# Rows of gathered edges taken from the count tables, jobs spread over three written-out hops, slots unpacked in halves

## What is computed

```python
h = maximum(layernorm(x), 0)
for i in range(10):                       # the hops
    agg = segment_sum(feat[src] * e[:, None], dst)
    feat = (0.9 * agg + 0.1 * h) * r[i] + (1 - r[i]) * feat
x = x + feat
emb = maximum(layernorm(x), 0)
for _ in range(4):                        # the GNN steps
    m = (emb @ W_msg.T + b_msg).reshape(n, 4, 128)
    r = segment_sum(m[src, etype], dst)
    emb = gru_cell(r, emb)
out = x + emb
```

## Time and profile before

| | us |
|---|---|
| median of three runs | 2313.57 (2311.01 to 2314.75) |
| the profiled execution | 2312.61, span 2311.1 |
| PE busy | 2077.3 (90%) |
| DVE busy | 1374.2 (59%) |
| POOL busy | 915.8 (40%) |
| ACT busy | 506.0 (22%) |

### The profile page before, as it was taken

One profiled execution on the slowest core, in us unless ns is written; L12 is line 12 of the kernel. 1 busy time (PEld: TensorE's weight loads), 2 busy tenths in 40 slices (PEclk: granted clock), 3 DMA queues, 4 the chain that ended last, 5 costly groups with the idle time before them and its releaser, 6 DMA issues.

```text
span 2311.1 us, 43556 instructions
## 1 busy us (share of the span) xinstructions
PE 2077.3 (90%) x15432; PEld 1452.2 (63%) x16039; DVE 1374.2 (59%) x2749; ACT 506.0 (22%) x1139; POOL 915.8 (40%) x1021
## 2 busy tenths in 40 slices
PE   3656666799999999999899999999999999999998
PEld 2333333699998989988755566555665556655566
DVE  8989898887776777777752245522455224552233
ACT  3888888300000000000121012210122101220001
POOL 4776775000000000000038870388703887038870
PEclk8665555699999999999999999999999999999999
DMA  2000000100000000001441110411104111043111
GB/s 80 23 24 34 24 34 30 45 1 1 2 2 2 1 2 1 2 2 60 126 125 39 39 44 3 125 40 39 44 3 126 40 39 44 2 127 66 40 44 31
DMA packets 62758, 90.05 MB, mean 39 GB/s; under 512 B 31953, under 2 KB 48927, under 8 KB 59654
## 3 DMA queue, kind: packets, MB, share of 16 engines
q1 hardware_dynamic: 21185, 54.88, 7.3%
q0 software_dynamic: 38400, 31.28, 5.8%
q10 hardware_dynamic: 2944, 0.93, 0.2%
HBM read 47.48 MB, written 39.05 MB: 37 GB/s over the span
## 4 chain that ended last, share of the span: by engine, by line
PE 43%; POOL 26%; DVE 16%; issue 9%; DMA 2%; ACT 2%; DVEq 1%; POOLq 1%; ACTq 0%; SPq 0%
PE ps L1033 26%; POOL big L513 24%; PE ps L938 11%; PE ps L822 2%; DVE m_full L1668 2%; DVE m_parts L1661 2%; PE ps L921 2%; DVE marks L1240 2%; DVE dig L1268 1%; DVE big L1270 1%; DMA messages_by_edge_kind<-m_parts 1%; PE ps L904 1%; POOL win_w L475 1%; DVEq L1227 1%; PE ps L866 1%
## 5 line engine op out<-in xcount | busy, mean ns | idle before, releaser
L513 POOL DMA_INDIRECT big<-messages_by_edge_kind,edge_row x480 | 641.4, 1336 | 1169.9 <-DMA messages_by_edge_kind<-m_parts 1024.8
L938 PE MATMUL ps<-slots,m_parts 125*128 125x436 fp8e4 (+1 forms) x5600 | 962.4, 330 | 4.0 <-DVE m_parts L1661 2.9
L938 PEld LDWEIGHTS ps<-slots,m_parts 125*128 125x128 f16 x5600 | 540.7, 98 | 360.1 <-issue 1.3
L1033 PE MATMUL ps<-parts,big 125*128 125x256 f16 x6125 | 673.2, 273 | 10.8 <-DVE parts L1457 4.4
L1033 PEld LDWEIGHTS ps<-parts,big 125*128 125x128 fp8e4 x6125 | 592.9, 98 | 65.2
L1545 DVE TENSOR_SCALAR slots<-big 128x2800 int32<-128x2800 int32 (+1 forms) x112 | 217.0, 1941 | 259.7 <-PE ps L938 253.3
L822 PE MATMUL ps<-hot_pair,weighed 125*128 125x228 f16 x1000 | 218.4, 369 | 140.8 <-ACT weighed L634 69.6
L822 PEld LDWEIGHTS ps<-hot_pair,weighed 125*128 125x128 f16 x1000 | 117.8, 123 | 241.1 <-ACT weighed L634 202.8
L634 ACT ACTIVATE weighed<-marks,win_w 125x128 f16<-125x128 f16 x625 | 194.7, 391 | 59.4 <-DVE marks L1240 58.9
L565 ACT ACTIVATE rs<-rs 125x25 f32<-125x25 f32 (+3 forms) x5 | 1.1, 216 | 712.0 <-DVE rs L1108 712.0
L1473 DVE SCALAR_TENSOR_TENSOR hop_tmp<-ps,coef,g 125x128 f32<-125x128 f32 x250 | 87.4, 350 | 94.0 <-PE ps L1033 90.2
(11 more groups left out here) (230 smaller groups left out, 1570.3 us busy)
## 6 DMA issues: line engine op xcount, KB each, us to landing
messages_by_edge_kind<-m_parts SPq DMA_DIRECT2D x20, 1120.0 KB
packed_counts<-packed SPq DMA_DIRECT2D x16, 625.0 KB, 2.9
big<-messages_by_edge_kind,edge_row POOLq DMA_INDIRECT x480
big<-packed_counts SPq DMA_DIRECT2D x4, 1400.0 KB, 6.4
big<-packed_counts SPq DMA_DIRECT2D x3, 1050.0 KB, 5.8
messages_by_edge_kind<-m_parts SPq DMA_DIRECT2D x20, 130.0 KB
hd<-in_x SPq DMA_DIRECT2D x1, 1562.5 KB
x_again<-in_x SPq DMA_DIRECT2D x1, 1562.5 KB
```

The source lines that it names most:

```text
L513: pool.indirect_dma_start(out=picked[0:CH, r, w, :, :].rearrange("p h f -> p (h f)"), out_offset=None, in_=m_dram[:, :], in_offset=bass.In ...
L938: last = pe.matmul(ps[:, k % 2, 0:SIZES[k] * QD], m_parts[0:Q, a, t, h, :], slots_f8[0:Q, t % 2, 0:SIZES[k], a, 0:QD], start=a == 0 and t ...
L1033: last = pe.matmul(ps[:, n % RING, 0:2 * F], tot_f8[0:Q, c, a, :], both((parts0, parts1)[par], a), start=a == 0, stop=a == TILES - 1)
```

## The change

The numbers for gathered edges are no longer made over all edges and turned. GpSimd stages key, place and weight of the eight pairs' columns instead (three small instructions a pair, in the room of `hot_to`), and `edge_parts`, 15 small instructions of VectorE, works source row and target out of them. GpSimd waits for the rows once ahead of its gathers (`s_rows`). The three window rows are turned and copied together. VectorE's loop covers hops 0 to 5; hops 6, 7 and 8 are written out and carry, in this order, `update_scales`, `edge_parts` and `mark_targets` (behind every second tile from tile 2). `unpack` issues two instructions, one for half of the block's tiles each; of three tiles the first takes one and the second two. Core of the diff:

```diff
-            hot_to = sb("hot_to", [128, PAIRS, GW, PC], U8, b)
+            hot_room = sb("hot_to", [128, PAIRS * GW * PC], U8, b)
...
+        hot_to = hot_room[:, :].rearrange("p (g w n) -> p g w n", g=PAIRS, w=GW)
+        hot_to_f8 = hot_room[:, :].bitcast(F8).rearrange("p (g w n) -> p g w n", g=PAIRS, w=GW)
+        near = hot_room[:, 0:5 * PAIRS * GW * 4].bitcast(F32).rearrange("p (j m) -> p j m", j=5)
+        near_key, near_place, near_weight, near_pair = (near[:, j, :] for j in range(4))
+        near_lane = near[:, 4, :].bitcast(I32)
...
-            pool.wait_ge(s_edges[1], 16)
-            pool.wait_ge(s_edges[2], 16)
-            pool.tensor_scalar(edge_g[0:ROWS, 0, :], edge_i[0:ROWS, 1, :], float(TYPES), None, ALU.mult).then_inc(s_grow4, 1)
-            pool.tensor_copy(edge_g[0:ROWS, 1, :], edge_i[0:ROWS, 2, :]).then_inc(s_grow4, 1)
-            pool.wait_ge(s_grow4, 2)
-            pool.tensor_tensor(edge_g[0:ROWS, 0, :], edge_g[0:ROWS, 0, :], edge_g[0:ROWS, 1, :], ALU.add).then_inc(s_grow, 1)
-            pool.wait_ge(s_grow, 1)
-            pool.wait_ge(s_edges[0], 16)
-            pool.tensor_copy(edge_g[0:ROWS, 1, :], edge_i[0:ROWS, 0, :]).then_inc(s_grow, 1)
-            pool.memset(edge_kind[:, NCH:PAD], 0)
-            pool.memset(edge_to[:, NCH:PAD], NOWHERE)
             pool.iota(iota_to[:, :], [[1, PC]], base=0, channel_multiplier=0, allow_small_or_imprecise_dtypes=True)
-            pool.iota(pair_off[:, :], [[PC, PAIRS]], base=TILES * QD, channel_multiplier=0, allow_small_or_imprecise_dtypes=True)
...
-            pool.wait_ge(s_gtab, 2)
             pool.wait_ge(s_pair, 1)
             for pair in range(PAIRS):
                 lo = pool.value_load(pair_lo[0:1, pair:pair + 1], min_val=0, max_val=NCH)
-                pool.tensor_copy(edge_row[0:CH, pair * GW:(pair + 1) * GW], edge_kind[0:CH, ds(lo, GW)])
-                pool.tensor_tensor(win_to[0:CH, pair * GW:(pair + 1) * GW], edge_to[0:CH, ds(lo, GW)],
-                                   pair_off[0:CH, pair:pair + 1].broadcast_to([CH, GW]), ALU.subtract).then_inc(s_to, 1)
+                at, q = slice(pair * GW, (pair + 1) * GW), QD + 2 * pair
+                pool.tensor_copy(near_place[0:CH, at], tab[0:CH, 0, ds(lo, GW)])
+                pool.tensor_copy(near_weight[0:CH, at], tab[0:CH, 1, ds(lo, GW)])
+                pool.tensor_tensor(near_key[0:CH, at], keys[0:CH, ds(lo, GW)], q_off[0:CH, q:q + 1].broadcast_to([CH, GW]),
+                                   ALU.subtract).then_inc(s_to, 1)
...
                 share_largest()
+                pool.wait_ge(s_rows, 1)
...
-            act.wait_ge(s_tr, 1)
-            cast(tab[0:CH, 0, 0:NCH], 0).then_inc(s_tabs, 1)
-            act.wait_ge(s_gtr, 1)
-            cast(edge_kind[0:CH, 0:NCH], 6).then_inc(s_gtab, 1)
-            act.wait_ge(s_tr, 3)
-            cast(tab[0:CH, 1, 0:NCH], 4).then_inc(s_tabs, 1)
+                ins.then_inc(s_tabs, 1)
...
-            act.wait_ge(s_gtr, 2)
-            cast(edge_to[0:CH, 0:NCH], 2).then_inc(s_gtab, 1)
...
-            pe.wait_ge(s_const, 2)
-            pe.wait_ge(s_key, 1)
-            turn_rows(edge_p[0:ROWS, 0, :], 0).then_inc(s_tr, 1)
-            pe.wait_ge(s_grow, 1)
-            turn_rows(edge_g[0:ROWS, 0, :], 6).then_inc(s_gtr, 1)
-            pe.wait_ge(s_key, 2)
-            turn_rows(edge_p[0:ROWS, 1, :], 2).then_inc(s_tr, 1)
-            pe.wait_ge(s_key, 3)
-            turn_rows(edge_p[0:ROWS, 2, :], 4).then_inc(s_tr, 1)
...
-            pe.wait_ge(s_grow, 2)
-            pe.wait_ge(s_keys, 1)
-            turn_rows(edge_g[0:ROWS, 1, :], 2).then_inc(s_gtr, 1)
             pe.wait_ge(s_win, 1)
-            for j in range(2):
-                last = pe.transpose(ps[0:1, 1, j * QB:(j + 1) * QB], lohi[0:QB, 2 * j:2 * j + 1], ident[0:QB, 0:QB])
+            for j, column in enumerate((0, 2, 1)):
+                last = pe.transpose(ps[0:1, 1, j * QB:(j + 1) * QB], lohi[0:QB, column:column + 1], ident[0:QB, 0:QB])
             last.then_inc(s_win_tr, 1)
-            pe.wait_ge(s_tabs, 2)
-            pe.transpose(ps[0:1, 4, 0:QB], lohi[0:QB, 1:2], ident[0:QB, 0:QB]).then_inc(s_win_tr, 1)
             pe.wait_ge(s_keys, 1)
             pe.wait_ge(s_tabs, 2)
-            pe.wait_ge(s_gtab, 2)
-            pe.wait_ge(s_win_hi, 1)
...
-            dve.tensor_copy(windows[0:1, 0:2 * QB], ps[0:1, 1, 0:2 * QB]).then_inc(s_win_row, 1)
-            dve.wait_ge(s_win_tr, 2)
-            dve.tensor_copy(windows[0:1, 2 * QB:3 * QB], ps[0:1, 4, 0:QB]).then_inc(s_win_hi, 1)
+            dve.tensor_copy(windows[0:1, :], ps[0:1, 1, 0:3 * QB]).then_inc(s_win_row, 1)
...
             def unpack(s, k, t):

                 u = TYPES * (BLOCKS * s + k) + t
-                n = SIZES[k % BLOCKS] * TILE_D // 4
-                first = START[k % BLOCKS] * TILE_D
+                size, first = SIZES[k % BLOCKS], START[k % BLOCKS] * TILE_D
                 dve.wait_ge(s_slot_free, u + 1)
                 if isinstance(s, int):
                     dve.wait_ge(s_pblk[k], 16)
-                TS(slots[:, t % 2, 0:n * 4].bitcast(I32).rearrange("p (n b w) -> p n b w", b=NBD, w=2),
-                   big1[:, first:first + n * 4].bitcast(I32).rearrange("p (b n w) -> p n b w", b=NBD, w=2),
-                   2 * t, LOWBITS, ALU.logical_shift_right, ALU.bitwise_and).then_inc(s_slot, 1)
+                for lo, hi in ((0, size // 2), (size // 2, size)):
+                    a, z = lo * TILE_D, hi * TILE_D
+                    last = TS(slots[:, t % 2, a:z].bitcast(I32).rearrange("p (n b w) -> p n b w", b=NBD, w=2),
+                              big1[:, first:first + size * TILE_D].bitcast(I32).rearrange("p (b n w) -> p n b w", b=NBD, w=2)
+                              [:, lo * TILES:hi * TILES, :, :],
+                              2 * t, LOWBITS, ALU.logical_shift_right, ALU.bitwise_and)
+                last.then_inc(s_slot, 1)
...
+            def edge_parts():
+
+                rel, place, weight, pair = near_key[0:CH, :], near_place[0:CH, :], near_weight[0:CH, :], near_pair[0:CH, :]
+                lane, kind, within = near_lane[0:CH, :], weight.bitcast(I32), win_to[0:CH, :]
+
+                def pairs_of():
+                    step(TS(kind, kind, 23, None, ALU.logical_shift_right))
+                    step(TS(pair, rel, 0.5 - KQ / 2, 1.0 / KQ, ALU.add, ALU.mult))
+                    step(TS(pair, pair, MAGIC, -MAGIC, ALU.add, ALU.add))
+
+                def rest_of():
+                    step(TS(kind, kind, -float(BASE_EXPONENT), 0.0, ALU.add, ALU.max))
+                    step(STT(out=rel, in0=pair, scalar=-float(KQ), in1=rel, op0=ALU.mult, op1=ALU.add))
+                    step(TS(lane, kind, 3, None, ALU.logical_shift_right))
+
+                def within_of():
+                    step(TS(within, rel, -float(TILES // 2), 1.0 / TILES, ALU.add, ALU.mult))
+                    step(TS(kind, kind, 7, None, ALU.bitwise_and))
+                    step(TS(within, within, MAGIC, -MAGIC, ALU.add, ALU.add))
+
+                def source_of():
+                    step(STT(out=rel, in0=within, scalar=-float(TILES), in1=rel, op0=ALU.mult, op1=ALU.add))
+                    step(STT(out=within, in0=lane, scalar=float(LANE), in1=within, op0=ALU.mult, op1=ALU.add))
+                    step(STT(out=rel, in0=kind, scalar=1.0 / 8, in1=rel, op0=ALU.mult, op1=ALU.add))
+
+                def rows_of():
+                    step(STT(out=rel, in0=place, scalar=float(TILES), in1=rel, op0=ALU.mult, op1=ALU.add))
+                    step(STT(out=within, in0=pair, scalar=float(TILES), in1=within, op0=ALU.mult, op1=ALU.add))
+                    TS(edge_row[0:CH, :], rel, float(TYPES), None, ALU.mult).then_inc(s_rows, 1)
+
+                return pairs_of, rest_of, within_of, source_of, rows_of
...
-                def hop(h, par, before, scales_at=None):
+                def hop(h, par, before, beside=None):

                     step(TS(coef[0:Q, :], inv_deg[0:Q, :], gain[0:Q, ds(h, 1)], None, ALU.mult))
                     for c in range(TILES):
                         dve.wait_ge(s_acc, before + c + 1)
                         hop_tile(step, ps[0:Q, (par * TILES + c) % RING, :], c, h, (parts1, parts0)[par],
                                  lambda: dve.sem_inc(s_ring, 1)).then_inc(s_parts, 1)
-                        if c == scales_at:
-                            update_scales(step)
-                        if scales_at and c >= TILES - PAIRS:
-                            mark_targets(c - (TILES - PAIRS))
-
-                with dve.Fori(0, HOPS // 2 - 1) as i:
+                        if beside:
+                            beside(c)
+
+                def scales_beside(c):
+                    if c == 3:
+                        update_scales(step)
+
+                def edges_beside(c):
+                    pieces = edge_parts()
+                    if c in range(3, 3 + len(pieces)):
+                        pieces[c - 3]()
+
```

(10 more changed lines are left out.)

31 lines of the change are left out of this document (14 added, 17 removed).

## The result

The changed kernel took 2287.14 us (median of 4 runs, 2286.62 to 2291.48); the kernel before, run beside it, 2314.16 (2311.01 to 2315.65). The ratio is 0.9887, with a 95% interval of 0.9875 to 0.9899: 1.1% faster, where 0.8% was forecast. The profiled execution took 2286.73 us (span 2285.2), against 2312.61: 25.9 us less, where the sum had 19.0.

What follows compares the result with a forecast made beforehand. VectorE's chain was taken to bound the time ahead of counting, TensorE the hops and GNN steps. 2312.6 - 7.3 - 4.4 - 7.6 + 0.3 = 2293.6, said as 2294 us, range 2290 to 2307.

Steps and rivals of the forecast that it cites:

- the sum: Whole kernel: profiled 2312.6 us less 7.3, 4.4 and 7.6, plus 0.3 of cost, gives 2293.6 us.
- Part 1: Setup: without GpSimd's four big edge-row instructions VectorE is no longer held off and counting starts earlier, net -7.3 us.
- The rival in which counting doesn't start earlier: Start of counting: another load or staging is late next, or counting changes rhythm; 2301 us, chance 0.10.
- Part 2: Last written-out hops: one VectorE job beside each hop removes TensorE's stalls at the next hop's start, gain 4.4 us.
- the lag: Hops: VectorE falls behind TensorE through the scales' 11.15 us, but in hop 6 catches up by its end.
- Gain 1.69 + 2.75 = 4.4 us, bounds 3.8 to 5: Start of hop 9: TensorE's two stalls of 1.69 and 2.75 us vanish because hop 8 carries only the one-hots.
- Part 3: GNN steps: unpacking in halves lets gathers through sooner, 5.9 us earlier per step, removing TensorE's 7.6 us of waits.
- All 7.6 us go: Four GNN steps: all 14 TensorE waits for gathered rows, 7.6 us together, disappear.
- the shelves: GNN steps: the four shelves for gathered lots would not become the next limit on the gathers.
- the 0.87 of my reading: Gathers: each needs VectorE's second port twice, some 0.13 and 0.87 us after its start.
- Its own range for the forecast: Whole kernel: 2290 to 2298 us if the main forecast of 2294 holds, chance 0.62.
- The 0.04: Whole kernel: chance 0.04 left for causes not thought of, fetching of the longer code above all.

Runs made afterwards that it cites:

- the two shifted kernels: The kernel before with 30 one-number memsets in the looped pair of hops: with the halved unpack 2304.84 us, without it 2313.64 us.
- the undone one: The changed kernel with each unpack one instruction again instead of two halves: 2299.66 us, 0.9925 of the kernel before.

## Why the prediction was right and wrong

**Part 1 was right:** -7.3 forecast, -7.36 in the trace. Reading rows 2 as VectorE held off, not working, was the decisive step, and the run with GpSimd's four instructions back shows it. Nothing else was late next. The 24 staging instructions and the wait for the row numbers cost nothing. The rival in which counting doesn't start earlier fell with it.

**Behind it, 0.8 us not forecast.** The start of the hops came 8.13 us earlier, not 7.36. Most of it may be scatter between profiles: the first pass, the 125 matmuls right ahead of the hops, took 16.48 us in the profile before and 15.63 after, and 15.24 to 16.48 over all traces here. It stays open.

**Part 2 failed in size.** The place and the lag that it named held: no stall at the start of hop 9, one of 0.60 in hop 6, nothing from the 15 instructions beside hop 7 or the one-hots beside hop 8. The failed step is "Gain 1.69 + 2.75 = 4.4 us, bounds 3.8 to 5". It priced a stall at its idle time and put what follows it at nothing. Undone, the part costs 7.5 us in the trace, because 1.8 to 2.7 us of slow matmuls, at 1.2 GHz for a part of them, follow such a stall each time; the 0.5 left is a seam. Rows 4 stopped seven matmuls behind the stall, and even these took 1.20 us, 0.17 each for 0.109. The same row read to its end, and the one at the seam behind hop 3:

```profile
714.53 138.30 PE L1033 MATMUL ps<-parts,big 125*128 125x256 f16 x1250 [1.97 <-issue]
...
1069.12 67.45 PE L1033 MATMUL ps<-parts,big 125*128 125x256 f16 x601 [2.75 <-DVE parts L1457]
```

65.7 us are due for the 601; the granted clock from 1069 to 1076 is 0.76. The other 1.7 us of the hops were the slow stretch at 714.53 (136.63 are due), of the kind that came in 11 of 21 seams.

**Part 3 failed in size too.** "All 7.6 us go" was right, but the term for it was the idle time of the matmuls, and the steps gave 10.0 (9.0 between the two shifted kernels, 11.9 in the undone one). The weight loads' waits were the better row. In the kernel before:

```profile
PEld L765 <- DMA big<-messages_by_edge_kind,edge_row: 9.6, 15, 1.1
```

The details hold. A gather caught at a start ended 2.02 us behind it, forecast 2.0. A pair takes 1.68 undisturbed (1.7 forecast), the three-tile halves cost the gathers some 2 us in a step (2.3 forecast), and the shelves didn't take over. What I had not counted is that a gather holds VectorE off too: of the pair at 1574.21 the first half took 1.29 us and the second 0.87. The kernel before has it as well:

```profile
1508.03 1.21 POOL L513 DMA_INDIRECT big<-messages_by_edge_kind,edge_row  x1 [0.30 <-issue]
...
1508.69 1.97 DVE L1545 TENSOR_SCALAR slots<-big 128x2800 int32<-128x2800 int32 x1
```

The 59 four-tile unpacks that began during a gather, in the kernel before and in its control with 30 memsets, fall into three groups without an exception. Begun up to 0.55 us behind the gather's start (32), the unpack took its 1.62 and the gather 2.19 to 2.50. Begun 0.60 to 0.99 behind it (17), the gather took its 1.21 and the unpack 1.64 to 2.03, as if it had been let in at 1.0. Begun later (10), neither was held. So a gather holds VectorE off only from about 0.6 to 1.0 us of its 1.21, and whoever comes first there goes first; the 0.87 of my reading lies in that stretch. The Trainium skill (SBUF — State Buffer, "Reading the diagram") lets whichever starts first keep the shared ports for its whole instruction. The 32 disagree: there the gather was first, was lengthened, and the unpack was not held.

**The range** failed with these two sizes. Its own range for the forecast, 2290 to 2298, let part 2 go to 5 us and part 3 to 7.6 at most. Both upper bounds on a gain were idle times of TensorE. With 6.2 for part 2 (4.4 and the 1.8 of slow matmuls behind it) and 9.6 for part 3, both from rows of the kernel before, the same sum is 2312.6 - 7.3 - 6.2 - 9.6 + 0.3 = 2289.8. The changed kernel's two medians are 2287.14 and 2289.77. Its first profile lies 3.1 lower, at 2286.7, by the 1.7 at a seam, the 0.8 ahead of the hops and some 0.7 more in the steps.

**The rivals.** None came. The 0.04 named "fetching of the longer code above all". Idle time at the turn of the step loop, 4.7 and 6.6 us of steps where the halves are put into the kernel before, may be of that kind; that fetching is its cause is not shown. The changed kernel happens not to have it. Which place calls it forth I can't say. Shown is that 60 instructions ahead of the loop take it away, at two positions, and that four in the changed kernel don't bring it.

## What to carry to other kernels

Price a stall of the bounding engine by the time until its instructions are back at their rate, not by the idle time: look at the row behind the gap and divide it by its count. For waits of TensorE set the weight loads' waits beside the matmuls'. And when a change alone gives less than undoing it costs, look for idle time that waits for nothing at the turns of loops, and move the loop by harmless instructions, with a control, before believing that the parts interact.
